# First attention layer of a four-layer block: probabilities turned by block transposes and DMA instead of TensorE, masks without matmuls, four heads' projections summed in PSUM

## What is computed

```python
q = (h @ Wq.T)                 # 32 heads of 128; rotated: q*cos + rotate_half(q)*sin
k = (h @ Wk.T)                 # 8 heads of 128, rotated likewise
v = (h @ Wv.T)                 # 8 heads of 128
scores = q_head @ k_group.T / sqrt(128)      # four q heads share one k and v head
scores = where(causal, scores, -inf)
attn = softmax(scores)
out = concat(attn @ v_group) @ Wo.T
```

## Time and profile before

| | |
|---|---|
| median of three runs | 2449.92 us |
| the profiled execution's own time | 2449.85 us |
| its span, first to last instruction | 2448.0 us |
| TensorE busy, of the span | 92% |
| VectorE, ScalarE, GpSimd busy | 66%, 55%, 54% |
| mean granted TensorE clock | 0.965 of full speed |
| first exponential of the first layer | 52.0 us |
| last addition of the first layer starts | 877.1 us |
| period of a group in the first layer | 102.4 us |
| period of a group in the second attention layer | about 144.8 us |

### The profile page before, as it was taken

How to read it: one execution, slowest core, us unless ns; L and a number is a source line. 1 busy time by engine, 2 the same in 40 slices (tenths; PEclk the granted TensorE clock), 3 DMA queues, 4 the chain that set the end, 5 groups by cost and what they waited for, 6 DMA issues and landing times. The chain is left out here.

```text
span 2448.0 us, 39997 instructions
## 1 busy us (share of the span) xinstructions
PE 2240.6 (92%) x11431; PEld 1866.0 (76%) x11431; DVE 1615.0 (66%) x2950; ACT 1337.8 (55%) x3605; POOL 1313.3 (54%) x1184
## 2 busy tenths in 40 slices
PE   4999999999999954799999999999999999855998
PEld 3888888888888843578888888888888888744887
DVE  4566665666666664378787777787887878755322
ACT  3666666666666633366656655655665665534321
POOL 3777777777777733355445455545545544324400
PEclk9999999999999986899999999999999999976999
DMA  2111111111111122044444334344334443333210
GB/s 79 52 40 53 43 47 47 43 51 43 47 47 44 39 65 84 12 121 108 113 106 106 103 97 116 100 111 113 99 94 110 108 112 85 98 99 114 82 44 26
DMA packets 141278, 189.63 MB, mean 77 GB/s; under 512 B 34992, under 2 KB 64848, under 8 KB 141040
## 3 DMA queue, kind: packets, MB, share of 16 engines
q1 hardware_dynamic: 141168, 188.39, 28.3%
HBM read 114.76 MB, written 6.42 MB: 50 GB/s over the span
## 5 line engine op out<-in xcount | busy, mean ns | idle before, releaser
L1339 ACT ACTIVATE l_probs<-l_score,l_negtop 128x512 f32<-128x512 f32 x256 | 175.1, 684 | 338.4 <-DVE l_negtop L1441 323.2
L207 POOL TENSOR_TENSOR l_probsT_lo<-l_moved,l_probsT_hi 128x512 fp32r<-128x512 f32 x128 | 183.0, 1438 | 243.9 <-ACT l_probsT_hi L1345 243.6
L808 DVE TENSOR_TENSOR acc<-l_out,acc 128x512 f32<-128x512 f32 x252 | 173.1, 687 | 131.3 <-PE l_out L202 129.0
L200 PE MATMUL l_score<-l_kT_lo,l_qT_hi 128*128 128x512 f32 (+3 forms) x512 | 204.4, 399 | 39.2 <-DVE l_kT_lo L1412 32.1
L671 ACT ACTIVATE l_probs<-l_score,l_negtop 128x128 f32<-128x128 f32 (+3 forms) x256 | 135.0, 527 | 191.0 <-DVE l_negtop L827 191.0
L200 PE MATMUL l_general<-l_w_qk_lo,xT_hi 128*128 128x512 f32 x512 | 201.5, 393 | 27.8 <-POOL l_w_qk_lo L207 27.8
L200 PE MATMUL l_out<-l_w_out_lo,l_oT_hi 128*128 128x512 f32 x508 | 217.9, 429 | 8.0 <-issue 3.5
L207 DVE TENSOR_TENSOR l_probsT_lo<-l_moved,l_probsT_hi 128x512 fp32r<-128x512 f32 x128 | 181.8, 1421 | 50.9 <-ACT l_probsT_hi L1345 50.9
L202 PE MATMUL l_general<-l_w_qk_hi,xT_hi 128*128 128x512 f32 x512 | 201.1, 393 | 0.0
L201 PE MATMUL l_general<-l_w_qk_hi,xT_lo 128*128 128x512 f32 x512 | 201.0, 393 | 0.0
L202 PE MATMUL l_out<-l_w_out_hi,l_oT_hi 128*128 128x512 f32 x508 | 200.0, 394 | 0.0
(11 more groups left out here) (216 smaller groups left out, 7015.8 us busy)
## 6 DMA issues: line engine op xcount, KB each, us to landing
l_moved<-l_blocks SPq DMA_DIRECT2D x1024, 64.0 KB, 2.0
l_stage<-l_wq SPq DMA_DIRECT2D x64, 256.0 KB, 2.6
l_stage<-l_wo SPq DMA_DIRECT2D x64, 256.0 KB, 2.6
l_inv_all<-inv_rows SPq DMA_DIRECT2D x64, 256.0 KB, 3.6
ffn_w_lo_words<-f_w SPq DMA_DIRECT2D x33, 256.0 KB, 2.8
l_raw_qk<-l_wq SPq DMA_DIRECT2D x64, 128.0 KB, 3.0
l_raw_qk<-l_wk SPq DMA_DIRECT2D x64, 128.0 KB, 3.1
l_raw_v<-l_wv SPq DMA_DIRECT2D x64, 128.0 KB, 2.9
```

Of the source, the lines that this page charges most:

```text
L200: nc.tensor.matmul(out, left.hi, right.lo, start=first, stop=False, skip_group_check=True)
L207: return engine.tensor_tensor(out, full, hi.bitcast(F32), ALU.subtract)
L808: dve.tensor_tensor(acc[:, row], out_of(m, j)[:], acc[:, row], ALU.add).then_inc(s_added, 1)
L1339: act.activation(probs[:, n % NPR], score[n % 2][:], ACT.Exp, bias=negtop[:, n:n + 1], accum_out=total[:, n:n + 1]).then_inc(s_exp, 1)
```

## The change

`attention_phase`, `Body` and their tables are deleted and `grouped_attention` takes their place in the first layer, on `Plan` and `Pass`, in the second layer's way, with these differences:

- **Two slots make a pair.** The causal triangle of an even slot and that of the next, odd slot lie interlocked in one array of 4 x 5 blocks for each of the 4 query blocks of 32 (`TRIANGLES`): the even slot's tile t fills column t + 1, rows 0 to t, the odd slot's tile t fills row t, columns 0 to t. One set of 16 DMAs, of 80 KB each, moves a pair (step 8 of the pair); the second layer has 16 of 64 KB for each slot.
- **Landing.** What landed is taken in four pieces of 512, 384, 256 and 128 elements a slot, from step 16: ScalarE makes all the high parts, VectorE the remainders of pieces 0 and 2, GpSimd those of 1 and 3. The value product (step 21 of the slot) reads them in blocks.
- **Mask and maximum in one.** There is no mask matmul. VectorE adds a mask from SBUF to the scores in PSUM, scales by -1/sqrt(128), writes them back and takes the minimum (`tops`).
- **No scaling of tiles on GpSimd.** Four reciprocals a group, of 8 columns each; the value product's result is multiplied by the inverses on VectorE, then split: the remainder now reads two SBUF tiles.
- **Output projection.** Four banks, one per tile of a slot, each summed over the four heads of a batch: 8 additions to the accumulator a group.
- **PSUM.** Two score banks, four output banks, two general banks, which the value products now share with q, k and v.
- **Weights.** q's and the output's four heads are loaded once a group (10 fetches and conversions in place of 18) into buffers that the remainders overwrite; VectorE makes the output weights' remainders, GpSimd the others.
- **Opening.** Before the first step k and two q are projected (before: k, v and its transposition, and one q).
- **Second layer.** The two semaphores of the inverses' DMAs become one; the inverses' DRAM rows get an array for each layer. `Pass.turns` gets a case that the first group of the new layer needs.

The diff, cut to its core:

```diff
-def attention_phase(p, ctx0, layer, xT, acc, ident, half, x_rows=None):
...
+MOVE0_AT, LAND0_AT, PV0_AT, OUT0_AT = 8, 16, 21, 25
+END0 = TILES + OUT0_AT
+USES0 = {("q", s): 4 * s - 8 for s in range(SLOTS)} | {("pv", s): 4 * s + PV0_AT for s in range(SLOTS)}
+USES0 |= {(kind, b): 16 * b + n for kind, n in (("k", -13), ("v", 11), ("vt", 14)) for b in range(B)}
+USES0 = Plan(USES0, lambda x: x[0] != "pv")
+OUTS0 = Plan({(s, t): 4 * s + t + OUT0_AT for s in range(SLOTS) for t in range(TB)})
+LOADS0 = {("wq", h): 4 * h - 13 for h in range(GH)} | {("wo", h): 4 * h + 21 for h in range(GH)}
+LOADS0 |= {("wk", 0): -19, ("wv", 0): 4}
+FETCH0 = Plan({x: n - 8 for x, n in LOADS0.items()})
+LOADS0 = Plan(LOADS0)
...
+def grouped_attention(p, ctx0, xT, acc, ident, half, x_rows, inv_rows):
...
+        score = p.banks(ctx, "l0_score", 2)
+        out_bank = p.banks(ctx, "l0_out", TB)
+        general = p.banks(ctx, "l0_general", 2)
+        NPR, NRAW, TRIANGLES = 2, 5, [P, 2, TB, TB, TB + 1, 32]
+        probs = sb("probs", [P, NPR, S])
+        blocks = sb("blocks", TRIANGLES)
...
+        def chunk_row(rows, slot, e):
+            return rows[:, :, e, e + 1:TB + 1] if slot % 2 == 0 else rows[:, :, TB - 1 - e, 0:TB - e]
+        def chunk_columns(rows, slot, k):
+            if slot % 2 == 0:
+                return rows[:, :, k, k + 1:TB + 1]
+            return rows[:, :, k:TB, k]
...
+        def landing(m, n):
+            for lag, pieces in ((LAND0_AT, (0, 1)), (LAND0_AT + 1, (2, 3))):
+                slot = m.slot_at(n, lag)
+                if slot is not None:
+                    for e in pieces:
+                        yield slot, e
+        def pair_at(m, n):
+            pair, rest_of = divmod(n - MOVE0_AT, PAIR)
+            return pair if rest_of == 0 and m.lagged(pair, SLOTS // 2) else None
...
+            def move(m, pair):
+                k, r = pair % 2, pair % (SLOTS // 2)
+                wait_past(sp, s_inv, m, SLOTS // 2, pair + 1)
+                sp.nop(nofuse=True)
+                wait_past(sp, s_inv_dma, m, 32 * (SLOTS // 2), 32 * pair)
+                sp.nop(nofuse=True)
+                sp.dma_start(inv_rows[k], inv[:, PAIR * r:PAIR * (r + 1)]).then_inc(s_inv_dma, 16)
+                wait_past(sp, s_block, m, TILES, PAIR * (pair + 1))
+                sp.nop(nofuse=True)
+                if not (m.first and pair < 2):
+                    was = 2 * pair - 3
+                    sp.wait_ge(s_free, m.done(USES0, ("pv", was % SLOTS), was // SLOTS))
+                    sp.nop(nofuse=True)
+                for g in range(TB):
+                    for c in range(TB):
+                        sp.dma_start(moved[32 * c:32 * c + 32, k, g],
+                                     blocks[32 * g:32 * g + 32, k, c]).then_inc(s_move[k], 16)
+                wait_past(sp, s_inv_dma, m, 32 * (SLOTS // 2), 32 * pair + 16)
+                sp.dma_start(inv_all[:, k], inv_rows[k].rearrange("p t -> (p t)").unsqueeze(0).to_broadcast([P, P * PAIR]))\
+                    .then_inc(s_inv_dma, 16)
...
+                if kind == "pv":
+                    slot = j + d * SLOTS
+                    if j % GH == 0:
+                        pe.wait_ge(s_free, m.done(USES0, ("vt", j // GH), d))
+                    wait_past(pe, s_lo_even, m, 2 * SLOTS, 2 * slot + 2)
+                    wait_past(pe, s_lo_odd, m, 2 * SLOTS, 2 * slot + 2)
+                    for k in range(TB):
+                        right = Split(chunk_columns(probsT_hi, slot, k),
+                                      chunk_columns(probsT_lo[:, slot // 2 % 2], slot, k))
+                        last = product(nc, by_block(bank[:])[:, :, k * 32:P].rearrange("p g (t i) -> p g t i", i=32),
+                                       v[:, j // GH, k * HD:(k + 1) * HD], right, k == 0, k == TB - 1)
...
+                if h == 0:
+                    wait_past(pe, s_added, m, B * TB, TB * (slot // GH + d * B - 1) + t + 1)
+                product(nc, out_bank[t][:], oT[:, slot % 2, t * P:(t + 1) * P], w_out[:, h], h == 0, h == GH - 1)\
+                    .then_inc(s_out, 1)
...
+            def exponentials(m, n):
+                t = n % TB
+                act.wait_ge(s_negtop, m.i * TILES + n + 1)
+                wait_past(act, s_block, m, TILES, n - NPR + 1)
+                act.activation(probs[:, n % NPR, 0:width[t]], score[n % 2][:, 0:width[t]], ACT.Exp,
+                               bias=negtop[:, n:n + 1], scale=-1.0, accum_out=total[:, n:n + 1]).then_inc(s_exp, 1)
+            def landed_hi(m, slot, e):
+                pair = slot // 2
+                if slot % 2 == 0 and e == 0:
+                    wait_past(act, s_move[pair % 2], m, SLOTS // 4 * MOVES, (pair // 2 + 1) * MOVES)
+                act.activation(chunk_row(probsT_hi, slot, e), chunk_row(moved[:, pair % 2], slot, e), ACT.Copy)\
+                    .then_inc(s_land_hi, 1)
...
+                    by = inv_all[:, pair % 2].rearrange("p (g i e) -> p e g i", g=TB, e=PAIR)
+                    last = dve.tensor_tensor(tokens(scaled[:]), by_token(bank[:]),
+                                             by[:, TB * (j % 2):TB * (j % 2 + 1)], ALU.mult)
...
+            def tops(m, n):
+                w = width[n % TB]
+                dve.wait_ge(s_score, m.i * TILES + n + 1)
+                dve.nop(nofuse=True)
+                dve.tensor_tensor_reduce(out=score[n % 2][:, 0:w], in0=score[n % 2][:, 0:w], in1=mask[:, S - w:S],
+                                         scale=-SCALE, scalar=3.0e38, op0=ALU.add, op1=ALU.min,
+                                         accum_out=negtop[:, n:n + 1]).then_inc(s_negtop, 1)
+            def inverses(m, pair):
+                r = pair % (SLOTS // 2)
+                wait_past(dve, s_exp, m, TILES, PAIR * (pair + 1))
+                at = slice(PAIR * r, PAIR * (r + 1))
+                dve.reciprocal(inv[:, at], total[:, at]).then_inc(s_inv, 1)
+            def turn_blocks(m, n):
+                slot, t = divmod(n, TB)
+                pair = slot // 2
+                wait_past(dve, s_exp, m, TILES, n + 1)
+                if n % PAIR == 0 and not (m.first and pair < 2):
+                    dve.nop(nofuse=True)
+                    wait_past(dve, s_move[pair % 2], m, SLOTS // 4 * MOVES, pair // 2 * MOVES)
+                rows = blocks[:, pair % 2]
+                to = rows[:, :, 0:t + 1, t + 1] if slot % 2 == 0 else rows[:, :, t, 0:t + 1]
+                dve.transpose(to.rearrange("p c k i -> p k c i"), probs[:, n % NPR, 0:width[t]]).then_inc(s_block, 1)
+            def landed_lo(m, slot, e):
+                wait_past(dve, s_land_hi, m, TILES, TB * slot + e + 1)
+                k = slot // 2 % 2
+                rest(dve, chunk_row(probsT_lo[:, k], slot, e), chunk_row(moved[:, k], slot, e),
+                     chunk_row(probsT_hi, slot, e)).then_inc(s_lo_even, 1)
+            def output_lo(m, slot):
+                wait_past(dve, s_o_hi, m, SLOTS, slot + 1)
+                rest(dve, oT.lo[:, slot % 2], scaled[:], oT.hi[:, slot % 2]).then_inc(s_o_lo, 1)
+            def out_weights(x, m, d):
+                dve.wait_ge(s_w_hi, m.done(LOADS0, x, d))
+                rest(dve, w_dest(x).lo, w_words(x), w_dest(x).hi).then_inc(s_w_out, 1)
+            def add_rows(m, x, d):
+                slot, t = x
+                dve.wait_ge(s_out, TT + m.done(OUTS0, x, d))
+                row = slot // GH * TB + t
+                dve.tensor_tensor(acc[:, row], out_bank[t][:], acc[:, row], ALU.add).then_inc(s_added, 1)
...
+            def landed_lo(m, slot, e):
+                wait_past(pool, s_land_hi, m, TILES, TB * slot + e + 1)
+                k = slot // 2 % 2
+                rest(pool, chunk_row(probsT_lo[:, k], slot, e), chunk_row(moved[:, k], slot, e),
+                     chunk_row(probsT_hi, slot, e)).then_inc(s_lo_odd, 1)
...
-        attention_phase(p, ctx, 0, xT, acc, ident, half, x_rows)
+        grouped_attention(p, ctx, xT, acc, ident, half, x_rows, inv_rows[0])
```

1003 lines of the change are left out of this document (349 added, 654 removed).

## The result

The changed kernel takes **2366.78 us** (median of 4 runs, 2359.91 to 2368.7); the kernel before took 2450.62 in the runs beside it (2448.22 to 2451.81). The profiled execution has a span of 2366.8 us, against 2448.0 before.

A forecast was written before the change was run, and what follows sets the result against it. TensorE was taken to bound the first layer at 102.4 us a group; 53 + 8 x 91 + 21 = 802 against 877.8 gave -76, so 2450 - 76 = 2374 us, range 2330 to 2428.

The forecast's parts named there:

- TensorE's need: First layer, per group: projections 55.0, scores and value products 29.8, transposes of v 0.9, together 85.7 us of TensorE work.
- Stalls: TensorE in the first layer's new pipeline: 4.9 us lost a group, taken from the second layer; 91 us a group taken.
- VectorE's sum: First layer: VectorE's instructions add up to 85 us a group, 73 uncontended, nearly as long as TensorE.
- The contention: VectorE's landed remainders: 1.426 us at 512 columns against 0.693, when GpSimd runs the other half at the same time.
- GpSimd and ScalarE: First layer, per group: GpSimd well under 77.9 us, ScalarE under 63.7, below the period of 91.
- The moves: SP queue, four a group: 10 us of issue and about 2 of flight hidden in 17 us, 5 to spare.
- The ends: First layer's start and finish: first exponential at 53 us, give or take 4, and 21 us beyond eight group periods.
- The drain term: First exponential to last addition of the first layer: 21 us more than eight periods; the second layer had 18.
- Unstalled: Rival: TensorE runs without stalls in the first layer, 86 us a group, 2331 us in all; chance 0.12.
- Shared banks: Rival: value products sharing two PSUM banks with q, k, v stall TensorE 11.4 us a group; 2422 us; chance 0.23.
- VectorE slower than before: Rival: two-SBUF-input operations all wait and VectorE bounds the first layer, 108 us a group; 2510 us; chance 0.08.
- Narrow runs in PSUM: Rival: value products' narrow runs are slow, 9.4 us a group, 100.4 in all; 2449 us, no change; chance 0.03.

The follow-up runs named there:

- kernel 2: The changed kernel with the mask matmul put back behind each score product, 32 a group; 2381.23 us, ratio 0.9711 to the kernel before.
- kernel 9: The changed kernel with the mask matmuls and 80 dummy transposes a group put back on TensorE; 2431.69 us, ratio 0.9922 to the kernel before.
- kernel 12: The changed kernel with the output weights' remainders moved from VectorE back to GpSimd; 2352.85 us, ratio 0.9606 to the kernel before.
- kernel 7: The changed kernel with value products and output projections one step later (22 and 26); 2424.2 us, ratio 0.9895 to the kernel before.
- kernel 3: The changed kernel with 32 unused one-column reciprocals a group added on VectorE, behind each maximum; 2372.63 us, ratio 0.9676 to the kernel before.
- kernel 11: The changed kernel with VectorE making all four landed remainders of a slot and GpSimd none; 2428.83 us, ratio 0.9921 to the kernel before.
- kernel 4: The changed kernel with every head added by VectorE, 32 additions a group instead of 8; 2412.34 us, ratio 0.9836 to the kernel before.
- kernel 10: The changed kernel with a pair's move issued at step 13 instead of 8; 2484.28 us, ratio 1.0133 to the kernel before.
- kernel 5: As kernel 4, but with two output banks and two banks for the value products alone; 2414.19 us, ratio 0.9844 to the kernel before.

## Why the prediction was right

The mechanism and the place came out as written, and so did the size of the period: 91.4 against 91 us a group, the gain in the first layer alone. Point by point:

- **TensorE's need.** 85.7 counted, 86.4 by the medians of its starts. Kernels 2 and 9 show that this work set the pace before: put back whole, TensorE is full again and 66 of 84 us return.
- **Stalls.** 4.9 was taken from the second layer, 5.0 was measured, or 4.5 to 6.1 by other ways to count. The size is right partly by luck, since the kinds are this layer's own: 3.4 us a group on banks that VectorE has to evacuate and 1.0 on exponentials. Kernel 12 takes the second kind away, kernel 7 multiplies the first.
- **VectorE's sum.** 85 forecast, 82.9 measured as a sum of durations, by terms: maxima 15.8 (15.4), their accumulator reads 4.5 (taken as none, bound 6.2), transposes 16.0 (15.5), landed remainders 12.7 (18.2), scaling 9.1 (8.4), output remainder 6.1 (7.5), output weights 3.0 (3.8), rotation, v and additions 15.0 (15.1), reciprocals 0.8. Two errors of 5 us cancel: the accumulator read is a second instruction, as the Trainium skill says (VectorE: DVE Perf Modes, Two Vector instructions with no wait between them), here of 140 ns; and the landed remainders lose 0.22 us each on the mean and not 0.73. The conclusion drawn from the sum, "nearly as long as TensorE", was wrong: durations of neighbours overlap, VectorE is busy for 70.07 of 91.4 us, and a group with 98.3 us of durations still runs in 94.0. What costs is not its sum but what stands ahead of a maximum or an evacuation without a wait of VectorE in between (kernels 3, 11 and 12; kernel 4 for the case with one).
- **The contention.** The row's range (0.693 to 1.733) held at 512 columns (0.679 to 1.041). Its cause, GpSimd's half of the landings, is right for these in 35 of 40 cases and too narrow for the rest: the pieces of 256 meet rotations, and kernel 11 shows rotations alone doing it. Each of the two engines waits for the instruction that the other has begun, which agrees with the Trainium skill (SBUF — State Buffer, Who interferes with whom): VectorE's 384 columns take 1.64 us instead of 0.55. Why the mean is 0.91 and not 1.43: VectorE starts in the middle of a GpSimd instruction of 1.0 us and waits for its rest only. In the changed kernel GpSimd pays as well, 1590 ns for 1288.
- **GpSimd and ScalarE** are at 63.84 and 58.40, below the period as said.
- **The moves.** 16 in 10.02 us, 2.1 us of flight, hidden. The spare time is 2.7, 7.1, 4.1 and 5.6 us for the four pairs of a group, the forecast's 5 in the mean; kernel 10 shows the price of having too little. The one wait of ScalarE for moved blocks, 5.9 us, is at the layer's last pair.
- **The ends.** The opening was 51.1 (53). The drain term is the one mis-sized: from the first exponential to the last addition the layer takes 8 x 91.4 + 11.3 us, not + 21. The first group is 76.6 us, 14.8 short of a period, as most of its value products and output projections are still to come (they come 21 and 25 steps of 32 behind their slot); and from the last group's start to the end there are 117.8, 26.4 more than a period. The second layer, from which the term came, has a like end (170.3 us, 25.5 more than its 144.8), but its first group is only 6.9 short: what the term of 21 missed is the short first group. The other stages had been taken as unchanged. So the first layer's end comes 8.4 us before the forecast's 802: -1.9 for the opening, +3.2 for the period (8 x 0.4), -9.7 for the drain. With +2.9 elsewhere the profiled execution takes 2368.55 us, and the median lies 1.8 below that.
- **The rivals.** *Unstalled* did not come, though kernel 12 goes 1.4 us towards it. *Shared banks* is the mechanism of the larger part of the stalls, at the six places that it named, but with 3.4 us a group and not 11.4: a wait is mostly the tail of an evacuation. Kernel 7 shows how near the larger price was: one step, 7.6 us. *VectorE slower than before* did not come; kernel 11 moves towards it with 16 more instructions and stops at 99.6. *Narrow runs in PSUM* cost nothing: value products of 384 columns start 0.176 us apart, of 256 0.118 and of 128 0.112, as in the earlier trace rows. The non-contiguous patterns against which the Trainium skill warns (PSUM — Partial Sum Buffer, the table's row on cachelines) show no price in these runs of 32 to 128 columns.

## What to carry to other kernels

When work comes off a full engine, its new pace is its own remaining work plus the short waits that the full queue had hidden; adding work back to it first fills those waits (here 13.2 us of work and switches cost 8.2 us). For the engines that feed it, don't compare sums of durations with the period: look at which of their instructions stand ahead of the one that it waits for, and whether the engine has a wait of its own in that step. Four instructions of 0.75 us a group moved out of a step of VectorE that had none were worth 1.4 us a group, while 24 additions, 15 us a group, most of them in steps where it had waited, cost 2.6. And in a pipeline written by steps, the one step by which two uses of a PSUM bank are apart is worth as much as a whole class of instructions (kernel 7).

## What the hardware showed that I had not expected

Kernels 4 and 5 change only the first layer, but the second became 20.7 us longer in both, 1199.4 against 1178.7 us from first exponential to last addition. From its third group on its groups take 147.4 to 150.4 us, where they take 142.6 to 147.9 in the changed kernel. The difference sits at the group boundaries, at two places. Ahead of the new group's first score product, the distance to the start before is 2.02 to 2.58 us at the five inner boundaries of kernel 4 (1.91 to 2.44 in kernel 5); in the changed kernel it is 2.90 and 2.72 us at two of them and under 1 at three, in kernel 12 under 1 at all five. Within the microseconds behind that product, the largest distance is 1.21 to 2.58 us in kernel 4 (0.87 to 2.18 in kernel 5), and at most 0.33 us in the changed kernel and in kernel 12. TensorE's timeline at one boundary of kernel 4:

```profile
1238.75 0.37 PE L85 MATMUL l_general<-l_w_v_hi,xT_hi 128*128 128x256 f32 x1 [2.08 <-issue]
...
1241.48 0.41 PE L83 MATMUL l_general<-l_w_v_lo,xT_hi 128*128 128x256 f32 x1
1241.70 0.41 PE L84 MATMUL l_general<-l_w_v_hi,xT_lo 128*128 128x256 f32 x1
...
1242.42 0.28 PE L83 MATMUL l_general<-l_w_v_lo,xT_hi 128*128 128x256 f32 x1
1242.54 0.29 PE L84 MATMUL l_general<-l_w_v_hi,xT_lo 128*128 128x256 f32 x1
```

And the windows view of two boundaries of that kernel (the clock is the third number from the end):

```profile
1236.00:1243.00 7.00, 4.92 (x27) 4.71 (x26) 4.14 (x6) 2.31 (x5) 6.92 (x6) 0.76 0.24 54
1386.00:1393.00 7.00, 6.21 (x29) 5.84 (x28) 3.73 (x6) 2.30 (x5) 6.92 (x6) 0.56 0.22 50
```

TensorE stands idle for 2.08 us, then runs at the lower of its two levels, 1.2 GHz, with starts of 256 columns 0.21 us apart, and goes back to 2.4 GHz and 0.12 us at about 1242. In the changed kernel one boundary shows such a stretch (at 1215 us), in kernel 4 four do (0.76 and 0.55 at the two not shown). Of the 20.7 us, 12.8 are time in which TensorE is idle (68.4 us in the second layer of kernel 4, 55.6 in the changed kernel, by the windows view); the other 8 agree with the lower clock behind it, 20.4 us of stretches at half speed against 3.4 at these boundaries. Why an unchanged layer waits longer at its boundaries stays open: the profile puts the wait shown down to "issue", which names no cause, and no run was made on it. It is why kernel 4's total says little about additions, and why the first layer's own marks were compared in every run.
